# A four-layer transformer kernel on one core: the order of its steps laid down alternately backwards and forwards

## The chip, the cores and the metric

One core of one Trainium2 chip runs the whole kernel as one program. The metric is the device time of one execution in microseconds (us). The kernel before took 1387.23 us in the median of three executions (1386.0 to 1388.7). The execution that was profiled took 1388.27 us.

## The reference, cut to what matters

The input is eight batches of 256 tokens with 288 channels. Four layers follow each other. Layers 0 to 2 are transformer blocks: a layer norm that is shifted and scaled by rows made from a condition vector, attention with 16 heads of 18 channels, a projection, a second such layer norm and an MLP. Layer 0 has four experts of which each token takes two, and all four are computed. Layer 1 mixes its heads in another layout. Layer 3 is a rotation: it needs the orthogonal factor of a QR decomposition of P and the exponential of a skew matrix, both independent of x.

```
mod = silu(c) @ w_adaln + b_adaln
h = (ln(x)) * (1 + sc_msa) + sh_msa
q, k, v = split((h @ w_qkv + b_qkv))
attn = softmax(q k^T * hd ** (-0.5));  o = attn v;  x = x + g_msa * (o @ w_proj + b_proj)
xn = (ln(x)) * (1 + sc_mlp) + sh_mlp
hmid = gelu(xn @ w1 + b1);  eo = hmid @ w2 + b2;  x = x + g_mlp * sum_e cw_e * eo_e
...
U, _ = qr(P);  R = expm(A(cond));  z = x @ U;  out = x + (z @ R - z) @ U^T
```

## The kernel before

The program is not written in the order in which it runs. Python generators (`prep`, `attend`, `finish`, `up`, `down`, `householder` and others) emit **steps** with `do(lane, kind, cost, ...)`. A lane is an engine: pe, dve, act, pool, or sp, the queue that issues nearly all transfers. A step is a few instructions of one engine, with a cost in the planner's own table and the list of steps that it depends on. The dependencies include the reuse of buffers and PSUM banks, which are dealt out while the steps are emitted, so they are fixed before any reordering.

When all 4,768 steps are known, `by_readiness` deals them out once more to the five lanes: again and again it takes the lane that could start a step soonest, and on a lane the step that is ready, with the lowest `index` where several are ready within 0.1 us. Here `index` is the place in the emitted order. Steps that raise the same semaphore keep their order, and so do all steps that use an activation table. The result is five fixed lists, and each engine works through its own in order; a step that is not ready holds up everything behind it on its engine.

The kinds that matter here. `ln_stats`, `ln_aggr` (dve, L1760 and L1765), `ln_eps`, `ln_pow`, `ln_mean` (pool, L2258 to L2269) and `ln_z` (act, L2112) are a layer norm; `xb_T` (pe, L1451 and L1452) turns it, and `full`, `m_hi`, `m_lo` (dve or act or pool; L1741 or L2106, L1747, L1754 to L1756) write it to `XT` in two f16 parts. `qkv_mm` (pe, L1424) and `up_mm` (pe, L1577, up to 14 matmuls) read `XT`. `top_mm` (pe, L1529) makes scores whose row maxima `top` reduces (dve, L1845, 16 for a batch); `top_T`, `top_out` and `top_row` (pe; act; sp, L2388) send them back as a row of `QT`, and only then can the scores `s_mm` (pe, L1544) start. `down_mm` (pe, L1584 to L1589) is the MLP's second product, in three pieces for each of four 128-token tiles n0 to n3; `down_gate` (dve, L1920) and `x_add` (pool, L2285) add it to x. `cond_mm`, `cond_add` and `cond_T` (pe L1441, dve L1699, pe L1434) make the condition's rows. `w_lo`, `w2_lo` (dve) split weights into two f16 parts. `w2_in` (sp, L2364) loads the second MLP weight and `w_keep` (sp, L2370) stores split weights. The QR decomposition is 64 rounds of `hh_row` (sp, L2331), `hh_norm` (act), `hh_root` (pool) and `hh_step` (dve, L1965 to L1971), each dependent on the one before; it is needed only near the end of layer 2.

Of the kernel before, what the change touches and what calls it, by code (L numbers as in the profile page):

```python
# [24 lines left out]
LAT, FILL, TAB = 0.08, 0.15, 1.3  # L25
SIZES = dict(x_in=295, w_in=442, cond_in=345, w2_in=442, w_back=1400, w_keep=1400, g1_in=147, g2_in=295, tv_in=295, tv_out=295, out=295, v_in=640, wp1_in=350, p_in=74, hh_row=37)
AHEAD = 3
NEAR = 0.1
LATE = ("dconsts",)
TABLES = dict(exps="exp", t_exp="exp", g_exp="exp", gelu="gelu", silu="silu")  # L30
SPLIT = {(2, 3): [(0,), (1,)]}
SLACK, BIAS = -0.5, 0.2


def flat(x):
    if x is None:
        return
    if isinstance(x, list):
        for y in x:
            yield from flat(y)  # L40
    else:
        yield x
# [14 lines left out]
def ends(x):  # L57
    return max((s.end for s in flat(x)), default=0.0)
# [79 lines left out]
def by_readiness(lanes, lands):  # L138


    queues, table = [], None
    for lane in lanes:
        some = {}
        for k, st in enumerate(lane.steps):
            st.index, st.end = k + 100000 * (st.kind in LATE), None
            name = "table" if st.kind in TABLES else id(st.sem)
            some.setdefault(name, deque()).append(st)
        queues.append(list(some.values()))
        lane.steps, lane.clock = [], 0.0
    while True:  # L150
        best = None
        for lane, some in zip(lanes, queues):
            mine = None
            for qu in some:
                if qu and all(x.end is not None for x in qu[0].deps):
                    begin = max(lane.clock, max((x.end for x in qu[0].deps), default=0.0) + LAT)
                    key = (begin if begin > lane.clock + NEAR else lane.clock, qu[0].index)
                    if mine is None or key < mine[0]:
                        mine = key, begin, qu
            if mine and (best is None or mine[1] < best[0]):  # L160
                best = mine[1], lane, mine[2]
        if best is None:
            return
        begin, lane, qu = best
        st = qu.popleft()
        if st.kind in TABLES and TABLES[st.kind] != table:
            table, begin = TABLES[st.kind], begin + TAB
        lane.clock = begin + st.cost
        st.end = lands(st, lane.clock)
        lane.steps.append(st)  # L170


def part(g, n):
# [12 lines left out]
def program(nc, I, out, scr_ada, scr_v, scr_o, scr_w1, scr_w2):  # L186
    ctx = ExitStack()
    with ctx:
# [5 lines left out]
        def sem(name):  # L194
            if name not in sems:
                sems[name] = ctx.enter_context(nc.semaphore("s_" + name))
                counts[name] = 0
            return sems[name]

        wire = Wire()  # L200

        def lands(st, at):
            return (wire.land(st.kb, at) + (2.0 if st.kind == "hh_row" else 0.0)) if st.kb else at + (FILL if st.lane is pe else 0.0)

        pe, dve, act, pool, sp = (Lane(n) for n in ("pe", "dve", "act", "pool", "sp"))
        newest = [0.0]

        def do(lane, kind, cost, raises=None, incs=1, **fields):
            name = raises or kind
            s = sem(name)  # L210
            st = Step(kind, s, counts[name], counts[name] + incs, fields)
            counts[name] += incs
            lane.clock = max(lane.clock, max((ends(v) for v in fields.values() if isinstance(v, (Step, list))), default=0.0) + LAT) + cost
            st.kb, st.lane = SIZES.get(kind, 8) if incs >= 16 else 0, lane
            st.end = lands(st, lane.clock)
            newest[0] = max(newest[0], st.end)
            st.cost, st.deps = cost, [x for v in fields.values() if isinstance(v, (Step, list, tuple)) for x in flat(v) if isinstance(x, Step)]
            lane.steps.append(st)
            return st
# [8 lines left out]
        table = [None]  # L228
# [116 lines left out]

        consts = do(pool, "consts", 3.2, incs=1)
        zeros = do(dve, "zeros", 0.4)
        xt_ones = do(pool, "xt_ones", 5.5, incs=7)
        dconsts = do(dve, "dconsts", 4.4, after=consts)
        c_in = do(sp, "c_in", 0.1, incs=16)  # L350

# [901 lines left out]
        class Stream:  # L1253


            def __init__(self):
                self.todo, order = [], [0, 1, 2, 3]
                for L in range(3):
                    for c in range(4):
                        for e in order if L == 0 else [0]:  # L1260
                            for vs in SPLIT.get((L, c), [(0, 1)]):
                                self.todo.append((L, e, c, vs))
# [115 lines left out]
        ends_ = Line(chain(*(chain(*[wp_load(L)] * (L > 0), *(chain(settle_tokens(b) if L == 1 else settle(L, b), finish(L, b)) for b in range(B))) for L in range(3))), 0.5)  # L1378
        deal([Line(householder(), 4), loads, attends, ends_, tops, preps, bg, *(Line(rotated(k), 5) for k in range(2))])

        wire.clock = 0.0
        by_readiness([pe, dve, act, pool, sp], lands)

# [1082 lines left out]
def make(nc, arrays):  # L2468
    args = {k: nc.dram_tensor(f"in_{k}", a.shape, mybir.dt.from_np(a.dtype), kind="ExternalInput").ap() for k, a in arrays.items()}
    out = nc.dram_tensor("out_0", (B * T, C), F32, kind="ExternalOutput").ap()  # L2470
    scr_ada = nc.dram_tensor("scr_ada", (3, B, 6 * C), F32, kind="Internal").ap()
    scr_v = nc.dram_tensor("scr_v", (B, 11 * C), F32, kind="Internal").ap()
    scr_o = nc.dram_tensor("scr_o", (B, T, C), F32, kind="Internal").ap()
    scr_w1 = nc.dram_tensor("scr_w1", (NE, 128, 5, HID), F16, kind="Internal").ap()
    scr_w2 = nc.dram_tensor("scr_w2", (NE, 128, 19, C), F16, kind="Internal").ap()
    program(nc, args, out, scr_ada, scr_v, scr_o, scr_w1, scr_w2)
# [11 lines left out]
```

## Time and profile before

| | |
|---|---|
| median of three executions | 1387.23 us |
| profiled execution: its time | 1388.27 us |
| profiled execution: span from first to last instruction | 1386.1 us |
| PE busy | 1296.8 us (94%) |
| DVE busy | 899.0 us (65%) |
| ACT busy | 784.3 us (57%) |
| POOL busy | 444.5 us (32%) |
| mean granted TensorE clock | 0.980 |

PE is the matmul engine, DVE the vector engine, ACT the scalar engine, POOL GpSimd, SP the queue of transfers. The clock is given as a share of full speed, so 0.5 is its lower level, 1.2 GHz of 2.4. The median is 1.04 us below the profiled execution.

### The profile page before, as it was taken

The page shows a single profiled execution, that of the slowest core. Times are in us where ns is not written, and L with a number is a line of the kernel's source. Part 1 is how long each engine was busy: PE and PEld are TensorE (multiplying, and loading weights), DVE is VectorE, ACT ScalarE, POOL GpSimd, SP SyncE. Part 2 cuts the span into 40 slices and gives each one's busy share as a digit, 9 for nine tenths or more (in the row PEclk, how much of TensorE's full clock was granted, in tenths as well). Part 3 has the DMA queues.
Part 4 walks back from the last instruction along what each step waited for, and adds up shares of the span by engine and source line. Part 5 has one row for each costly group of instructions (what it writes and reads, how often), then busy time and mean ns, then how long its engine had stood idle before and what let it go on. Part 6 is the DMA issues. An engine that isn't in the chain of part 4 may idle for free.

```text
span 1386.1 us, 33182 instructions
## 1 busy us (share of the span) xinstructions
PE 1296.8 (94%) x13225; PEld 946.5 (68%) x13225; DVE 899.0 (65%) x1983; ACT 784.3 (57%) x1565; POOL 444.5 (32%) x817
## 2 busy tenths in 40 slices
PE   5687999999999899999998999899998999999998
PEld 3343756777777688777887778787675767676775
DVE  5787887767686574666537654675665855776454
ACT  3665558677666342455337344666454676756653
POOL 4122425335243432323433333223331314231210
PEclk9788999999999999999999999999999999999999
DMA  8413154554543323232324323322000020000001
GB/s 232 114 31 73 38 145 115 141 143 121 144 98 70 89 58 86 32 69 94 94 49 75 69 57 123 99 41 66 5 14 2 14 56 3 14 6 15 2 29 52
DMA packets 81935, 96.20 MB, mean 69 GB/s; under 512 B 40077, under 2 KB 74998, under 8 KB 78454
## 3 DMA queue, kind: packets, MB, share of 16 engines
q1 hardware_dynamic: 81510, 93.79, 27.5%
q8 instruction: 105, 1.72, 0.5%
q14 instruction: 48, 0.39, 0.1%
q10 hardware_dynamic: 272, 0.29, 0.1%
HBM read 73.22 MB, written 16.38 MB: 65 GB/s over the span
## 4 chain that ended last, share of the span: by engine, by line
PE 74%; DVE 12%; issue 5%; ACT 3%; DMA 3%; POOL 3%; SPq 1%; DVEq 0%; POOLq 0%; ACTq 0%
PE P L1577 18%; PE P L1424 12%; PE P L1587 7%; PE P L1589 7%; PE P L1588 7%; DVE NM L1845 5%; PE P L1553 4%; PE P L1544 2%; PE P L1520 2%; PE P L1451 2%; DMA QT<-MT 1%; PE P L1441 1%; PE P L1598 1%; PE P L1464 1%; PE P L1584 1%
## 5 line engine op out<-in xcount | busy, mean ns | idle before, releaser
L1577 PE MATMUL P<-XT,W 128*128 128x256 f16 x3024 | 351.5, 273 | 6.6 <-ACT FULL L2106 3.6
L1577 PEld LDWEIGHTS P<-XT,W 128*128 128x128 f16 x3024 | 289.8, 98 | 57.0 <-issue 12.6
L2285 POOL TENSOR_TENSOR X<-X,TM 128x288 f32<-128x288 f32 x144 | 124.3, 865 | 497.6 <-DVE TM L1920 352.4
L1587 PE MATMUL P<-W,H 128*128 128x288 f16 x864 | 247.5, 286 | 0.0
L1589 PE MATMUL P<-W,H 128*128 128x288 f16 x864 | 247.1, 286 | 0.0
L1588 PE MATMUL P<-W,H 128*128 128x288 f16 x864 | 247.1, 286 | 0.0
L2192 ACT ACTIVATE G<-P 128x512 f32<-128x512 f32 (+1 forms) x240 | 133.2, 555 | 171.7 <-PE P L1577 163.2
L2181 ACT ACTIVATE ARENA<-P 128x512 f32<-128x512 f32 x256 | 135.1, 599 | 72.7 <-PE P L1544 72.1
L1845 DVE TENSOR_REDUCE NM<-P 128x2 f16<-128x512 f32 x256 | 159.5, 686 | 11.8 <-PE P L1529 11.4
L1424 PE MATMUL P<-WQ,XT 128*128 128x288 f16 x1008 | 145.6, 296 | 11.3 <-DVE XT L1756 5.1
L2290 POOL TENSOR_TENSOR H<-G,H 128x512 f16<-128x512 f32 (+1 forms) x97 | 105.7, 1095 | 128.5 <-ACT H L2193 126.2
L2193 ACT ACTIVATE H<-P 128x512 f16<-128x512 f32 (+1 forms) x240 | 132.7, 553 | 0.0
L1914 DVE TENSOR_TENSOR H<-G,H 128x512 f16<-128x512 f32 (+1 forms) x143 | 92.0, 654 | 61.7 <-ACT H L2193 60.9
L1424 PEld LDWEIGHTS P<-WQ,XT 128*128 128x128 f16 x1008 | 96.7, 101 | 47.8 <-issue 18.9
L1587 PEld LDWEIGHTS P<-W,H 128*128 128x128 f16 x864 | 84.5, 98 | 25.9 <-issue 5.2
L1589 PEld LDWEIGHTS P<-W,H 128*128 128x128 f16 x864 | 84.5, 98 | 21.3
L1588 PEld LDWEIGHTS P<-W,H 128*128 128x128 f16 x864 | 84.6, 98 | 20.6
L2301 POOL TENSOR_SCALAR N<-HQS 64x1 f32<-64x1 f32 x64 | 19.0, 296 | 183.4 <-ACT HQS L2198 183.2
L2198 ACT ACTIVATE HQS<-HQS 64x288 f32<-64x288 f32 (+31 forms) x64 | 26.4, 413 | 86.4 <-DMA HQS<-AT 86.2
L1553 PE MATMUL P<-ARENA,V 128*32 128x256 f32 x1024 | 70.4, 392 | 3.7 <-ACT ARENA L2181 3.5
L1920 DVE SCALAR_TENSOR_TENSOR TM<-P,CW,G 128x288 f32<-128x288 f32 x64 | 32.7, 511 | 59.0 <-PE P L1589 59.0
L2106 ACT ACTIVATE FULL<-P,SC 128x256 f32<-128x256 f32 (+1 forms) x93 | 44.9, 558 | 39.9 <-PE P L1452 39.5
(304 smaller groups left out, 2132.8 us busy)
## 6 DMA issues: line engine op xcount, KB each, us to landing
W<-scr_w SPq DMA_DIRECT2D x9, 1440.0 KB, 6.2
W<-scr_w SPq DMA_DIRECT2D x9, 1368.0 KB, 6.0
scr_w<-W SPq DMA_DIRECT2D x4, 1440.0 KB, 5.9
scr_w<-W SPq DMA_DIRECT2D x4, 1368.0 KB, 5.8
STG<-in_L_w SPq DMA_DIRECT2D x8, 576.0 KB, 4.8
STG<-in_L_w SPq DMA_DIRECT2D x9, 432.0 KB, 3.4
STG<-in_L_WT SPq DMA_DIRECT2D x11, 324.0 KB, 4.4
G<-scr_ada SPq DMA_DIRECT2D x24, 144.0 KB, 3.0
```

The costliest lines, as they stand in the source:

```text
L1424: ins = e.matmul(o, l, r, start=k == 0, stop=k == len(pairs_) - 1)
L1553: ins = e.matmul(bank(st)[32 * i:32 * i + 32, at], V32[u][:, kt, 4 * g + i, :], E32[s][:, i, kt * 256:(kt + 1) * 256], start=kt == 0, stop ...
L1577: ins = e.matmul(bank(st)[:, 256 * k:256 * k + 256], W1[:, w, m * 128:(m + 1) * 128], XT[:, x, at:at + 256], start=i == 0, stop=i == 6)
L1587: e.matmul(o, hi, W2[:, 2 * m, :], start=False, stop=False)
L1588: e.matmul(o, hi, W2[:, 2 * m + 1, :], start=False, stop=False)
L1589: ins = e.matmul(o, lo, W2[:, 2 * m, :], start=False, stop=m == 8)
L1845: e.tensor_reduce(NM[:, :, st["par"], st["c"]], bank(st).rearrange("p (n k) -> p n k", n=2), AX.X, ALU.max, negate=True).then_inc(st.sem)
L2181: e.activation(E32[st["s"]][:, st["h"], :], bank(st), ACT.Exp).then_inc(st.sem)
L2192: e.activation(g32, bank(st)[:, 0:n], fn, scale=1.0 / WS)
L2193: e.activation(hi, bank(st)[:, 0:n].rearrange("p (m t) -> p m t", t=256), fn, scale=1.0 / WS).then_inc(st.sem)
L2285: e.tensor_tensor(X[:, t, :], X[:, t, :], TM[st["k"]][:, :], ALU.add).then_inc(st.sem)
L2290: e.tensor_tensor(lo, g32.rearrange("p (m t) -> p m t", t=256), hi, ALU.subtract).then_inc(st.sem)
```

## The change

The single call of `by_readiness` is replaced by `improved`. It lays the steps down forwards as before, then `from_the_end` lays the same steps down backwards: it begins with steps on which nothing waits, and gives each step an `index` that says how far from the end it stands at the latest. The next forward pass takes these as its `index`. There are twelve forward passes, and the five lists of the pass with the shortest planned length on pe are kept. `xt_ones` gets `consts` as a dependency; on pool it stands behind it in both kernels. No step's content, cost or buffer changes.

```diff
+TIMES = 12
...
-            st.index, st.end = k + 100000 * (st.kind in LATE), None
+            st.end = None
...
-        st.end = lands(st, lane.clock)
+        st.end, st.done = lands(st, lane.clock), lane.clock
...
+def from_the_end(lanes):
+    queues, then, late = [], {}, {}
+    for lane in lanes:
+        some = {}
+        for st in reversed(lane.steps):
+            name = "table" if st.kind in TABLES else id(st.sem)
+            some.setdefault(name, deque()).append(st)
+            for x in st.deps:
+                then.setdefault(id(x), []).append(st)
+        queues.append(list(some.values()))
+    clocks = [0.0] * len(lanes)
+    while True:
+        best = None
+        for k, some in enumerate(queues):
+            mine = None
+            for qu in some:
+                if qu and all(id(x) in late for x in then.get(id(qu[0]), [])):
+                    st = qu[0]
+                    begin = max(clocks[k], max((late[id(x)] + LAT + st.end - st.done for x in then.get(id(st), [])), default=0.0))
+                    key = (begin if begin > clocks[k] + NEAR else clocks[k], -st.done)
+                    if mine is None or key < mine[0]:
+                        mine = key, begin, qu
+            if mine and (best is None or mine[1] < best[0]):
+                best = mine[1], k, mine[2]
+        if best is None:
+            return
+        begin, k, qu = best
+        st = qu.popleft()
+        clocks[k] = late[id(st)] = begin + st.cost
+        st.index = -clocks[k]
+
+def improved(lanes, lands, wire):
+    for lane in lanes:
+        for k, st in enumerate(lane.steps):
+            st.index = k + 100000 * (st.kind in LATE)
+    best = None
+    for _ in range(TIMES):
+        wire.clock = 0.0
+        by_readiness(lanes, lands)
+        if best is None or lanes[0].clock < best[0]:
+            best = lanes[0].clock, [list(lane.steps) for lane in lanes]
+        from_the_end(lanes)
+    for lane, steps in zip(lanes, best[1]):
+        lane.steps, lane.clock = steps, best[0]
...
-        xt_ones = do(pool, "xt_ones", 5.5, incs=7)
+        xt_ones = do(pool, "xt_ones", 5.5, incs=7, after=consts)
...
-        wire.clock = 0.0
-        by_readiness([pe, dve, act, pool, sp], lands)
+        improved([pe, dve, act, pool, sp], lands, wire)
```

The first forward pass of `improved` is the order of before, and the lists that come out differ, so a later pass was kept. Of the 1,498 steps on pe 1,075 keep their place and the others move by 1.7 places on average. On dve the mean over all steps is 5.4 places, above all because the 64 `hh_step` move 52 places later on average. On sp the `hh_row` move 8 places later. Line numbers of the changed kernel are 50 higher.

**Place 1, dve, the program's start.** In the kernel before, behind the constants (OSM is the first `cond_add`, ST and MV a layer norm's statistics, WQ weight splits of `w_lo`):

```order
L1699 SCALAR_TENSOR_TENSOR OSM<-P,PLUS,STG 64x288
L1760 BN_STATS ST<-X 128x6
L1705 SCALAR_TENSOR_TENSOR WQ<-STG,WQ 128x288
L1705 SCALAR_TENSOR_TENSOR WQ<-STG,WQ 128x576
L1765 BN_AGGR MV<-ST 128x2
L1760 BN_STATS ST<-X 128x6
L1705 SCALAR_TENSOR_TENSOR WQ<-H,WQ 128x288
L1705 SCALAR_TENSOR_TENSOR WQ<-H,WQ 128x576
L1712 SCALAR_TENSOR_TENSOR WQ<-H,WQ 64x288
L1765 BN_AGGR MV<-ST 128x2
```

In the changed kernel, from the same place:

```order
L1810 BN_STATS ST<-X 128x6
L1815 BN_AGGR MV<-ST 128x2
L1810 BN_STATS ST<-X 128x6
L1815 BN_AGGR MV<-ST 128x2
L1749 SCALAR_TENSOR_TENSOR OSM<-P,PLUS,STG 64x288
L1755 SCALAR_TENSOR_TENSOR WQ<-STG,WQ 128x288
L1755 SCALAR_TENSOR_TENSOR WQ<-STG,WQ 128x576
L1755 SCALAR_TENSOR_TENSOR WQ<-H,WQ 128x288
L1755 SCALAR_TENSOR_TENSOR WQ<-H,WQ 128x576
L1762 SCALAR_TENSOR_TENSOR WQ<-H,WQ 64x288
```

The statistics of the first batch now stand ahead of the first condition rows and of all weight splits.

**Place 2, sp, the first batch's maxima row.** In the kernel before (HQS is `hh_row`, the two QT rows are `top_row`, H is `w2_in`):

```order
L2378 DMA G<-scr_ada 128x288
L2383 DMA G<-scr_ada 128x2x288
L2331 DMA HQS<-AT 64x1x287
L2388 DMA QT<-MT 1x8x256
L2389 DMA QT<-MT 1x8x256
L2364 DMA H<-in_L_w 128x3x288 x2
```

In the changed kernel:

```order
L2398 DMA scr_ada<-OSM 8x288
L2381 DMA HQS<-AT 64x1x288
L2414 DMA H<-in_L_w 128x3x288 x2
L2438 DMA QT<-MT 1x8x256
L2439 DMA QT<-MT 1x8x256
L2414 DMA H<-in_L_w 128x3x288
```

The second `hh_row` has gone from ahead of the maxima row, and two loads of the MLP's second weight have come ahead of it.

**Place 3, pe, where layer 0's expert loop goes from tokens 512 to 1023 to the next quarter.** In the kernel before the last pieces of `down_mm` run one behind the other, then:

```order
L1589 MATMUL P<-W,H 128x288
L1451 MATMUL P<-IDF,ARENA 128x128 x2
L1452 MATMUL P<-IDF,ARENA 32x128
L1451 MATMUL P<-IDF,ARENA 128x128 x2
L1452 MATMUL P<-IDF,ARENA 32x128
L1587 MATMUL P<-W,H 128x288
L1588 MATMUL P<-W,H 128x288
L1589 MATMUL P<-W,H 128x288
L1577 MATMUL P<-XT,W 128x256 x14
L1424 MATMUL P<-WQ,XT 128x288 x42
```

In the changed kernel three of the five `up_mm` of the last half stand behind the `down_mm` of n0 and n1, ahead of those of n2:

```order
L1638 MATMUL P<-W,H 128x288
L1639 MATMUL P<-W,H 128x288
L1627 MATMUL P<-XT,W 128x256 x35
L1634 MATMUL P<-W,ONES 128x288
L1637 MATMUL P<-W,H 128x288
```

and `xb_T` stands ahead of all of n3:

```order
L1639 MATMUL P<-W,H 128x288
L1501 MATMUL P<-IDF,ARENA 128x128 x2
L1502 MATMUL P<-IDF,ARENA 32x128
L1501 MATMUL P<-IDF,ARENA 128x128 x2
L1502 MATMUL P<-IDF,ARENA 32x128
L1634 MATMUL P<-W,ONES 128x288
L1637 MATMUL P<-W,H 128x288
```

Between the end of n1, on which the layer norm depends, and `xb_T`, 35 matmuls of `up_mm` were added. The same stands at the next two quarters, the last time with 49 matmuls and with the following `up_mm` moved behind the projections of layer 1.

## Rows read from the trace of the kernel before

**Rows 1.** Windows: busy us of each engine (instructions), granted clock, DMA share, GB/s.

```profile
0.00:35.00 35.00, 19.37 (x130) 11.18 (x132) 20.14 (x59) 12.69 (x27) 14.43 (x40) 1.00 0.85 230
35.00:145.00 110.00, 81.22 (x773) 44.12 (x768) 87.68 (x187) 67.43 (x134) 26.13 (x61) 0.81 0.30 69
145.00:460.00 315.00, 304.96 (x3113) 220.35 (x3112) 232.40 (x522) 214.07 (x427) 130.62 (x230) 1.00 0.45 112
460.00:1000.00 540.00, 521.68 (x5747) 411.00 (x5745) 328.87 (x736) 258.92 (x537) 175.85 (x353) 1.00 0.30 70
1000.00:1386.00 386.00, 369.57 (x3473) 259.86 (x3471) 229.92 (x481) 231.21 (x442) 97.44 (x133) 0.99 0.06 19
```

**Rows 2.** Timeline, DVE, 0 to 50 us: start, us, what, [idle before <- releaser].

```profile
10.36 0.51 DVE L1699 SCALAR_TENSOR_TENSOR OSM<-P,PLUS,STG 64x288 f32<-64x288 f32 x1 [3.03 <-PE P L1441]
...
14.25 0.18 DVE L1765 BATCH_NORM_AGGREGATE MV<-ST 128x2 f32<-128x6 f32 x1
...
35.11 9.65 DVE L1845 TENSOR_REDUCE NM<-P 128x2 f16<-128x512 f32 x16
```

**Rows 3.** Timeline, POOL, 0 to 50 us.

```profile
14.52 0.79 POOL L2258 TENSOR_SCALAR NMS<-MV 128x2 f32<-128x2 f32 x1 [3.61 <-DVE MV L1765]
...
16.46 0.20 POOL L2269 TENSOR_TENSOR RS<-NMS,RS 128x2 f32<-128x2 f32 x1
```

**Rows 4.** Timeline, PE, 0 to 150 us.

```profile
7.23 3.09 PE L1441 MATMUL P<-STG,CS 96*32 96x288 f32 x12 [7.23 <-DMA STG<-in_L_w_adaln]
...
17.89 0.69 PE L1451 MATMUL P<-IDF,ARENA 128*128 128x128 f32 x2 [6.32 <-ACT ARENA L2113]
...
19.36 3.10 PE L1441 MATMUL P<-H,CS 96*32 96x288 f32 x12
...
24.42 4.26 PE L1424 MATMUL P<-WQ,XT 128*128 128x288 f16 x21 [0.83 <-issue]
...
82.86 1.46 PE L1544 MATMUL P<-QT,KT 64*128 64x256 f16 x12 [2.97 <-DMA QT<-MT]
...
104.75 0.44 PE L1451 MATMUL P<-IDF,ARENA 128*128 128x128 f32 x2 [1.31 <-DVE ARENA L1862]
...
119.00 1.84 PE L1424 MATMUL P<-WQ,XT 128*128 128x288 f16 x7 [2.19 <-DVE XT L1756]
```

**Rows 5.** Chain that ended last, 0 to 60 us: start, us, what.

```profile
46.86 0.48 SPq L2331
...
47.44 0.73 SPq L2388
...
48.21 3.47 DMA QT<-MT
```

**Rows 6.** Transfers issued, 0 to 60 us: KB of each, us to landing.

```profile
H<-in_L_w SPq DMA_DIRECT2D x3, 432.0 KB, 5.0
```

**Rows 7.** The page, part 6: transfers issued.

```profile
scr_w<-W SPq DMA_DIRECT2D x4, 1440.0 KB, 5.9
```

**Rows 8.** Timeline, DVE, 100 to 120 us.

```profile
101.09 1.06 DVE L1723 SCALAR_TENSOR_TENSOR W<-H,W 128x864 f16<-128x864 f32 x1
...
116.29 0.44 DVE L1965 CUSTOM_DVE_ANT_0 HQS<-HQS,AT 64x284 f32<-64x284 f32 x1
...
117.52 0.68 DVE L1754 TENSOR_TENSOR XT<-FULL,XT 128x512 f16<-128x512 f32 x1
```

**Rows 9.** Waits of PE, 150 to 1000 us: total, times, longest.

```profile
PE P L1577 <- ACT FULL L2106: 3.6, 3, 1.3
PE P L1424 <- DVE XT L1756: 2.9, 3, 1.2
...
PE P L1464 <- issue: 1.7, 1, 1.7
```

**Rows 10.** Timeline, POOL, 555 to 580 us.

```profile
564.39 0.79 POOL L2285 TENSOR_TENSOR X<-X,TM 128x288 f32<-128x288 f32 x1 [1.73 <-DVE TM L1920]
```

**Rows 11.** The page, part 5, the largest group: busy, mean of one.

```profile
L1577 PE MATMUL P<-XT,W 128*128 128x256 f16 x3024 | 351.5, 273 | 6.6 <-ACT FULL L2106 3.6
```


## The prediction, on record before the changed kernel ran

> **What bounds the kernel now.** I read the windows first. PE is busy 1296.8 of 1386.1 us, and its idle time by stretch is span minus busy [rows 1]: 15.6 us up to 35, 28.8 us from 35 to 145, 10.0 to 460, 18.3 to 1000 and 16.4 to the end, 89.2 us in all. So PE sets the time nearly everywhere, half of what it loses lies in the first 145 us, and a new order can give back only idle time and what the clock loses. The same rows show the clock: 0.81 from 35 to 145, 0.99 to 1.00 elsewhere. At 81.2 us busy, the share below the full level is worth 15.4 us.
>
> Then I read PE's timeline and what ends its waits. Between 35 and 145 us DVE is busy 87.7 of 110 us, more than PE, and 9.65 us of it is one block of row maxima [rows 1, 2]. There PE waits for maxima, for the row that comes back by DMA (2.97 us) and for `XT` parts from DVE (2.19 us) [rows 4]. Behind 145 us the waits are few; those of a kind are three for `FULL`, 3.6 us, and three for `XT`, 2.9 us [rows 9], each pair at one crossing from one group of 512 tokens to the next in layer 0.
>
> **The change part by part.** Nothing is added or taken from any engine, so each term is a wait that shrinks or appears.
>
> *The start.* DVE idles 3.03 us up to 10.36 waiting for PE's first `cond_mm`, with the first batch's statistics behind it; these end at 14.25+0.18 [rows 2]. POOL stands idle 3.61 us up to 14.52 and needs until 16.66 for its three steps [rows 3]; PE waits 6.32 us up to 17.89 for what comes out [rows 4]. Place 1 puts the statistics ahead, into DVE's idle time. POOL is then free at 10.91 (14.52-3.61), and its 2.14 us end at 13.05, 3.6 us earlier. I take 3.0, since `ln_z` now stands behind `cond_cols` and a weight split on ACT. The first `cond_mm` gets a 432 KB load ahead of its bias: at the stretch's 230 GB/s [rows 1] up to 1.9 us later. It needed until 10.32, so until 12.2, and its columns are wanted only once `xb_T` has run, at about 16. That cover hides it. Next, `m_lo` of this batch stands behind the second `cond_add` now, which must wait for `cond_mm` to end at 22.46 (19.36+3.10) [rows 4]; in the new order it stands ahead. From `xb_T` at 17.89 to the first `qkv_mm` at 24.42 it takes 6.5 us; without that wait about 5.1. Together the projections start 4.4 us earlier; `cond_T` now stands among them (0.5 us), so the first maxima come 3.9 us earlier. Bounds: 1.5 (only `ln_z` moves, half) to 5.0.
>
> *The first maxima row.* `hh_row` holds the queue for `hh_step` until 46.86 and the row is issued at 47.44 [rows 5]. The change takes that `hh_step` and `hh_row` away from there (up to 0.7 us gained), but puts two `w2_in` ahead of the row (Place 2), 432 KB each. The row lands 3.5 us after its second half is issued; behind 864 KB at 230 GB/s it would wait up to 3.8 us more, less the head start of the loads. A 432 KB load needs 5.0 us by itself [rows 6], much of it no bandwidth. I take a loss of 1.0, bounds -0.7 and 3.8; one `qkv_mm` more stands ahead of the scores and fills part of it. Sum so far 2.9 us gained.
>
> The Trainium skill, "DMA: Bandwidth & Descriptors", section "Queues, rings and completion order", says that on each DMA engine descriptors are consumed in ring order. By that rule the row would bear the full 3.8 us, and the first maxima's 3.9 us would be spent up to here; no row of this trace has a small row directly behind such loads.
>
> *The second and third batch, 65 to 120 us.* DVE is the limit here. Of the second block of maxima the new order takes out one `hh_step` (1.2 us, as 116.29 to 117.52 [rows 8]) and an `x_lo`, and puts in a `w2_lo` (1.06 us, as at 101.09 in the same rows); I set the last two against each other: 1.2 us gained. Ahead of the third block an `hh_step` leaves the place before `av_rec`, for which PE waits 1.31 us at 104.75, and the next leaves the place before `m_lo` (117.52), for which PE waits 2.19 us at 119.00 [rows 4, 8]; `m_lo` also comes before a `proj_gate`. At most 1.31 and 1.6: I take 2.5. Two `w_keep` now stand ahead of two maxima rows in the queue, 1440 KB and 5.9 us each [rows 7]; both are ready some 15 us before those rows, which hides them; uncovered, each costs up to 5.9 us. With less idle time some of the 15.4 us of clock comes back; I take 2.0 (0 to 5), in proportion to a fifth of the 28.8 us of idle time less, rounded down. The head gives 2.9+1.2+2.5+2.0 = 8.6, say 9 us since two moves were set at nothing, bounds 1 and 14.
>
> *The three crossings in layer 0.* At the first, the last `x_add` of the tile pair runs at 564.39 [rows 10], and from there the layer norm, `xb_T`, `FULL` and `XT` are late for PE by 1.2 and 1.2 us. Place 3 puts 35 matmuls of `up_mm` between this chain's start and PE's need, at 351.5/3024 = 0.116 us each [rows 11] 4.1 us: more than the 2.4 us that were missing. The third crossing gets 49 of them, and the 1.7 us wait [rows 9] may go too. The sum of the waits is 3.6+2.9 = 6.5 us, 8.2 with the last. Against it, `down_mm` of n2 now follows directly on the last `up_mm`, whose `gelu` and `h_lo` were covered by n0 and n1 before; its first piece reads only early parts, and I allow 0.4 us for each crossing. Gain 5.0 us, bounds 1 and 8.
>
> *Everywhere else* steps have moved by one to three places on PE, and `hh_step` stands later on DVE, `hh_norm` on ACT. The decomposition then ends later, but PE needs its result only near the end of layer 2, and `v_T` there keeps its place; some 200 us remain. The 10.0, 16.4 and remaining 11.8 us of idle time can shrink or grow. The planner's durations are not the chip's, and a tighter order has less play: I take 1.0 us lost, bounds -8 and 6.
>
> Sum: 9+5-1 = 13 us. Against the profiled execution 1388.27-13 = 1375.3, its span 1373.1; the median is 1.04 us lower, so **1374 us**.
>
> **The rivals.**
>
> *Half of it is given back*: the early start is met by the queue (Place 2), and a small wait appears at each crossing where `h_lo` is late. For it speaks that ACT and DVE deliver each `up_mm` only just in time. Head 4, crossings 3: 1387-7 = 1380 us.
>
> *Nothing comes of it*: PE's work between 145 and 460 us waits for weight loads that start no earlier, so that an early head turns into a wait there. The DMA share is 0.45 at 112 GB/s, and PE idles only 10.0 of 315 us [rows 1]: against it, since loads are not the limit now. 1386 us.
>
> *More*: the scattered waits close as well and the clock holds its full level through the head (8 us of 15.4 back): 1387-13-10 = 1364 us.
>
> *Slower*: the large transfers moved ahead of the first three maxima rows. If the two `w2_in` cost 3.8 us and each `w_keep` its full 5.9 us, that is 15.6 us, and the clock costs as it does now in that stretch, 15.4 us for 28.8 us of idle time, so 8 us more. With the other head gains (3.9+1.2+2.5) and the crossings (5) that leaves 1387+23.6-12.6 = 1398 us. It decides when a `w_keep` is issued less than 6 us before a maxima row. Against it: only three of the 24 such rows got a larger transfer ahead of them.
>
> The Trainium skill, "TensorE: Matmul & The Clock Gate", Part 1, says the clock follows how busy the array has been; the trace agrees as far as it goes, with 0.81 in the stretch where PE idles 26% and 1.00 where it idles 3%.
>
> **How the numbers follow.** The forecast of 13 us has 0.50, half of it 0.24, nothing 0.10, more 0.09, slower 0.07. The forecast's own range is 1367 to 1380. The whole range of 1364 to 1384 leaves out the slower case, nothing, and a little beyond the case of more. A measurement of this kernel can tell about 0.2% (2.8 us) from no change, that is below 1384.4 or above 1390.0. Faster: 0.50+0.23+0.09 = 0.82; within: 0.10+0.01 = 0.11; slower: 0.07.
>
> **What would show it.** The first `qkv_mm` starts near 20 us instead of 24.42, the first block of maxima near 31 instead of 35.11. Idle time of PE from 35 to 145 us is near 23 instead of 28.8 and the clock is above 0.83. The three waits for `FULL` with `XT` behind them are gone or under 0.5 us. The scores of the first batch start near 49 us; if they start at 51.7 or later, the loads ahead of the row took the gain. The prediction is wrong if new waits at the `down_mm` behind an `up_mm`, or of `s_mm` for `QT`, add up to more than 5 us, or if PE's idle time behind 145 us shrinks by more than 15.

## The result, and the profile after

The changed kernel takes 1352.26 us (median of 4 executions, 1350.45 to 1354.26) against 1387.97 for the kernel before on the same chip (4 executions): a ratio of 0.9745, 95% interval 0.9725 to 0.9764. It is 36 us faster; 13 were forecast, and the time lies outside the range. The profiled execution took 1351.46 us, its span is 1349.7 us against 1386.1, the mean granted clock 0.989 against 0.980.

The changed kernel's windows, cut as in [rows 1] (us, busy of PE, its weight loads, DVE, ACT, POOL; clock, DMA share, GB/s):

```profile
0.00:35.00 35.00, 21.32 (x149) 11.52 (x149) 23.48 (x65) 12.88 (x31) 13.81 (x40) 1.00 0.85 225
35.00:145.00 110.00, 82.19 (x820) 49.92 (x821) 86.07 (x189) 70.51 (x137) 22.45 (x53) 0.88 0.31 78
145.00:460.00 315.00, 310.68 (x3265) 225.03 (x3266) 235.09 (x523) 214.09 (x423) 127.55 (x232) 1.00 0.47 117
460.00:1000.00 540.00, 534.21 (x5836) 418.65 (x5829) 344.95 (x761) 270.19 (x561) 189.52 (x367) 1.00 0.29 67
1000.00:1349.00 349.00, 335.98 (x3169) 237.94 (x3166) 215.28 (x450) 215.35 (x414) 87.73 (x126) 1.00 0.07 20
```

PE's idle time (span less busy) is 13.7, 27.8, 4.3, 5.8 and, with the last 0.7 us of the span, 13.7 us: 65.3 in all against 89.2, 24 less. PE's busy time is 12.4 us less (1284.4 against 1296.8). Most of that is the clock: in the stretches at the lower level PE was busy for 39.4 us before and for 19.0 us after, and half of each, 19.7 and 9.5 us, is what the level cost, so 10.2 less. Idle and busy time together are the 36. The profiled pair shows a large share for the clock: the four executions of the changed kernel were granted 0.984 to 0.989, and the kernel before, profiled at 0.980, was granted 0.979 to 0.984 in its executions beside the later runs, mostly 0.982 or 0.983. What does not fit the forecast is already seen here: the stretch from 35 to 145 us, where half the gain was expected, idles nearly as long as before (27.8 against 28.8 us), and the two stretches from 145 to 1000 idle 18.2 us less.

Fixed cuts mix a gain with the work that it moved. So the next windows are cut in both kernels at the same `up_mm` matmuls (the first one where the first scores for the maxima start, since no `up_mm` has run by then). First before, then after:

```profile
34.60:144.30 109.70, 80.92 (x776) 43.97 (x774) 87.31 (x186) 67.43 (x134) 26.13 (x61) 0.81 0.31 69
144.30:274.00 129.70, 122.89 (x1185) 87.00 (x1185) 101.38 (x224) 86.44 (x164) 52.51 (x91) 0.99 0.44 115
274.00:445.70 171.70, 170.06 (x1797) 124.54 (x1795) 119.12 (x275) 117.95 (x238) 68.55 (x127) 1.00 0.47 117
445.70:502.20 56.50, 51.57 (x613) 36.87 (x610) 36.45 (x90) 20.76 (x50) 21.41 (x42) 0.97 0.33 82
...
953.30:1143.80 190.50, 180.54 (x1764) 129.36 (x1761) 124.53 (x246) 114.72 (x213) 55.05 (x78) 0.98 0.07 18
1143.80:1386.00 242.20, 233.39 (x2138) 164.48 (x2135) 139.72 (x307) 142.79 (x281) 60.01 (x86) 1.00 0.06 17
```

```profile
31.50:136.80 105.30, 76.25 (x773) 43.78 (x773) 82.45 (x173) 66.92 (x132) 20.77 (x51) 0.87 0.32 81
136.80:257.30 120.50, 119.80 (x1185) 86.64 (x1184) 95.60 (x217) 85.71 (x160) 49.06 (x81) 1.00 0.46 123
257.30:429.00 171.70, 169.59 (x1797) 124.96 (x1795) 125.67 (x282) 120.10 (x242) 68.97 (x131) 1.00 0.49 118
429.00:479.20 50.20, 48.70 (x582) 34.74 (x581) 33.98 (x76) 19.21 (x45) 18.44 (x37) 1.00 0.32 90
...
924.10:1106.40 182.30, 178.47 (x1765) 127.89 (x1762) 127.20 (x254) 116.07 (x216) 54.10 (x82) 1.00 0.08 19
1106.40:1349.70 243.30, 232.47 (x2138) 164.25 (x2135) 141.77 (x309) 142.11 (x281) 60.01 (x86) 1.00 0.05 17
```

The gain of a segment is the difference of its second column. The start (0 to 34.6 in the kernel before, 0 to 31.5 after) gained 3.1 us and the head 4.4; from 144 to 274 us 9.2; nothing to 446; 6.3 to 502; 8.2 from 953 to 1144; nothing from there on. The stretch left out, 502 to 953 us before and 479 to 924 after, holds the three crossings of layer 0 and gained 6.2. The sum is 36.3 (the last segment lost 1.1). Two of these segments do not hold the same work: 32 small matmuls `P<-EY` stand ahead of the cut at 502 in the kernel before and behind it (479) in the changed one, as the counts 613 and 582 show, and they are worth some 1.4 us. So about 5 of the 6.3 us are a gain (3.4 of idle time, 1.6 of clock), and the crossings gained 7.6: their idle time fell from 12.6 to 4.9 us.

The waits of PE in the second segment, before (total, times, longest), and after, where these two lines are all:

```profile
PE P L1544 <- DVE LG L1871: 1.8, 1, 1.8
PE P L1577 <- DVE NM L1845: 1.5, 1, 1.5
PE P L1553 <- ACT ARENA L2181: 1.2, 3, 0.5
PE P L1561 <- ACT OT L2173: 0.7, 1, 0.7
```

```profile
PE P L1634 <- ACT ARENA L2231: 0.3, 1, 0.3
PE P L1634 <- DVE NM L1895: 0.2, 1, 0.2
```

None of these had been counted singly in the forecast: small waits, each another line's. (Idle time in this segment fell by 6.1 us, from 6.8 to 0.7; the clock gave 1.4 of the 9.2, and the other 1.7 stand in the profile as less busy time of PE.) The group of [rows 11] in the page after shows that the three waits for `FULL` are gone:

```profile
L1627 PE MATMUL P<-XT,W 128*128 128x256 f16 x3024 | 352.1, 273 | 0.3 <-DVE NM L1895 0.2
```

The head, as in [rows 4]: PE's timeline of the changed kernel from the start (start, us, what, idle before and its releaser):

```profile
9.31 3.09 PE L1491 MATMUL P<-STG,CS 96*32 96x288 f32 x12 [9.31 <-DMA STG<-in_L_b_adaln]
15.38 0.69 PE L1501 MATMUL P<-IDF,ARENA 128*128 128x128 f32 x2 [1.71 <-ACT ARENA L2163]
...
20.64 4.36 PE L1474 MATMUL P<-WQ,XT 128*128 128x288 f16 x21 [0.69 <-issue]
...
48.02 0.83 PE L1594 MATMUL P<-QT,KT 64*128 64x256 f16 x12
...
101.24 0.44 PE L1501 MATMUL P<-IDF,ARENA 128*128 128x128 f32 x2 [1.27 <-DVE ARENA L1912]
...
106.71 0.66 PE L1501 MATMUL P<-IDF,ARENA 128*128 128x128 f32 x2 [3.28 <-DVE NM L1895]
...
114.38 1.88 PE L1474 MATMUL P<-WQ,XT 128*128 128x288 f16 x14 [1.07 <-DVE XT L1806]
```

`cond_mm` starts 2.1 us later than in the kernel before, `xb_T` 2.5 us earlier, the first `qkv_mm` 3.8 us earlier.

### The profile page after: what moved, and what is told of

Same layout as the page of the kernel before. It is cut to its first block, busy times and chain, and to the rows that moved or that the text cites. A ratio compares the mean times of both kernels' runs of the same rounds, so it can differ in the third digit from the quotient of the medians.

```text
span 1349.7 us, 33186 instructions
## 1 busy us (share of the span) xinstructions
PE 1284.4 (95%) x13225; PEld 943.1 (70%) x13225; DVE 904.9 (67%) x1983; ACT 783.0 (58%) x1565; POOL 441.1 (33%) x817
## 4 chain that ended last, share of the span: by engine, by line
PE 80%; DVE 8%; ACT 4%; issue 3%; DMA 2%; POOL 1%; SPq 1%; DVEq 0%; ACTq 0%; POOLq 0%
PE P L1627 21%; PE P L1474 13%; PE P L1637 7%; PE P L1639 7%; PE P L1638 7%; DVE NM L1895 4%; PE P L1603 4%; PE P L1501 2%; PE P L1594 2%; PE P L1570 2%; PE P L1491 2%; PE P L1579 1%; PE P L1648 1%; PE P L1634 1%; PE P L1557 1%
## 5 line engine op out<-in xcount | busy, mean ns | idle before, releaser
L1627 PEld LDWEIGHTS P<-XT,W 128*128 128x128 f16 x3024 | 289.1, 98 | 48.6 <-issue 10.2
L1895 DVE TENSOR_REDUCE NM<-P 128x2 f16<-128x512 f32 x256 | 159.3, 685 | 14.4 <-PE P L1579 13.9
L1964 DVE TENSOR_TENSOR H<-G,H 128x512 f16<-128x512 f32 (+1 forms) x143 | 95.5, 680 | 51.2 <-ACT H L2243 50.3
```

The costliest lines, as they stand in the source:

```text
L1627: ins = e.matmul(bank(st)[:, 256 * k:256 * k + 256], W1[:, w, m * 128:(m + 1) * 128], XT[:, x, at:at + 256], start=i == 0, stop=i == 6)
L1895: e.tensor_reduce(NM[:, :, st["par"], st["c"]], bank(st).rearrange("p (n k) -> p n k", n=2), AX.X, ALU.max, negate=True).then_inc(st.sem)
```

## The experiments

Twelve kernels, each beside the kernel before on the same chip. "Gained" is always measured between the same `up_mm` matmuls against the kernel before, by the cuts above. The segments are those of the one profiled execution, the times the median of four to ten. Lines of these kernels lie a few further down than in the changed one. A round of the decomposition is counted where its `hh_step` starts: by the end of the head (144.3 us in the kernel before, 136.8 in the changed one) the kernel before has run 6 and the changed one 4, by the next cut (274 and 257.3) 15 and 11.

**1. Two passes in place of twelve.** Is it the rule, or the best of twelve draws?

```diff
-TIMES = 12
+TIMES = 2
```

> TIMES = 2: one backward pass and one forward pass behind it, instead of twelve forward passes. Theory A (the gain is in the rule itself, that a step is ranked by how far from the end it must stand): nearly all of the 35.7 us is there, 1352 to 1356 us. Theory B (the gain comes from trying many orders and keeping a lucky one): a good part is missing, 1365 us or more.

Measured 1358.5 us, ratio 0.9774 (0.9747 to 0.98), above the range of theory A by 2.5 us and far from theory B. One backward pass gives 30 of the 36 us, in the same places: 8.1 us from 144 to 274, 6.0 to 502.

**2. Only the decomposition later.** The forward pass of before, with the Householder kinds behind everything else that is ready.

```diff
-LATE = ("dconsts",)
+LATE = ("dconsts", "hh_row", "hh_norm", "hh_root", "hh_step")
...
-TIMES = 12
+TIMES = 1
```

> The order of before with one thing changed: the householder's steps (hh_row, hh_norm, hh_root, hh_step) get the last rank, so that they run only where nothing else is ready. Theory H (the householder's steps stood in the way of DVE, ACT, POOL and sp in the order of before, and moving them away is the gain): 1360 us or less. Rival (the gain needs the ranks of all steps): at most a few us, 1380 to 1388. My own terms for the head (hh_step out of three places and one hh_row) would give about 4 us, 1384.

Measured 1385.42 us, ratio 0.9970 (0.9956 to 0.9984). It gains 3.8 us in the head and 0.7 from 144 to 274, where the waits of 1.8 us for `LG` and 1.5 for `NM` stand as before. By the cut at 274 it has run 12 rounds, about as few as the changed kernel (11). So the rival came true: making the decomposition lazy does not by itself give the gain.

**3. The changed kernel with the decomposition first.** Its lists dealt once more with the Householder steps ahead of all.

```diff
+        for lane in (pe, dve, act, pool, sp):
+            for k, st in enumerate(lane.steps):
+                st.index = k - 100000 * st.kind.startswith("hh_")
+        wire.clock = 0.0
+        by_readiness([pe, dve, act, pool, sp], lands)
```

> The changed kernel with one thing undone: in its final order the householder's steps get the first rank again, so that each runs as soon as it can; all other steps keep their ranks. Theory H: most of the gain is lost, 1370 us or more. Rival: PE keeps what it has, since DVE, ACT and POOL are 65%, 58% and 33% busy, 1352 to 1358.

Measured 1374.02 us, ratio 0.9884 (0.9861 to 0.9907), 22 us slower than the changed kernel, as theory H had it. By the matmul that the changed kernel reaches at 257.3 it has run 22 rounds instead of 11 and is 14.9 us behind. Its windows to there:

```profile
31.30:143.10 111.80, 81.09 (x775) 45.53 (x775) 93.13 (x209) 69.11 (x144) 30.15 (x81) 0.81 0.40 80
```

```profile
143.10:272.20 129.10, 122.61 (x1183) 86.87 (x1183) 103.57 (x236) 87.06 (x170) 57.34 (x109) 0.98 0.48 117
```

DVE is 10.7 and 8.0 us busier than in the changed kernel and the clock is back at 0.81. Yet the crossings and the stretch from 953 to 1144 keep their gain, and 4.8 of the 6.3 us before 502 stay: those are not the decomposition's. This run does not undo the change, though: with 11 rounds in the head and 22 by the second cut it is far ahead of the kernel before too (6 and 15). It shows what eleven rounds too many cost, not what the four that the changed kernel puts off are worth.

**4. New order at the front, old behind it.** Each list is cut at 150 us of the plan's own time.

```diff
+    for lane, a, b in zip(lanes, best[1], old):
+        lane.steps = [st for st in a if ends_new[id(st)] < 150.0] + [st for st in b if ends_new[id(st)] >= 150.0]
```

> The new order for the first 150 us of the plan, the order of before for all that is left. If the gain of each stretch is its own, only the head's 7.5 us remain, and 1380 us comes out. If the new head hands work over so that the next stretch (145 to 274 us, 9.1 us gained there) runs better in the old order too, it is 1371 us or less. If the seam costs a wait, 1382 to 1386.

Measured 1403.36 us, ratio 1.0101 (1.0086 to 1.0116). The front gains 2.6 and 4.2 us as in the changed kernel; then comes one wait at the seam,

```profile
PE P L1582 <- ACT KT L2221: 17.3, 1, 17.3
```

which is far more than the seam was expected to cost (1403 us against 1382 to 1386). Behind it, from 502 to 1025 us, each segment is within 0.1 us of the kernel before. PE arrives there 14 to 16 us late, not early, so the run does not show whether an early head helps later; it shows that the old lists take their old time wherever they start.

**5 and 6. PE's new list with the helpers by the old order, and the reverse.** One list is kept as it is, the others are dealt out again around it by the other kernel's ranks.

```diff
+            name = "pinned" if lane.name in pinned else "table" if st.kind in TABLES else id(st.sem)
...
+    for lane, a, b in zip(lanes, best[1], old):
+        for k, st in enumerate(b):
+            st.index = k
+        lane.steps = a if lane.name in ("pe",) else b
+    by_readiness(lanes, lands, ("pe",))
```

(The second has `old` and `best[1]` exchanged.)

> PE's list is that of the changed kernel, word for word; the other four lanes are dealt out by the ranks of before. Theory P (the gain is in PE's own order, the helpers have room): 1352 to 1360 us. Theory J (the ranks pay only on all engines together, since PE meets each result as soon as the helpers' order brings it): most of the gain is lost, 1375 us or more.

> The reverse: PE's list is that of before, word for word; the other four lanes are dealt out by the ranks of the changed kernel. Theory P: no gain, about 1388 us. Theory J: no gain either and perhaps a loss, 1385 to 1397. Theory H (moving the helpers' work off the critical places is the gain): 1370 us or less.

Measured 1385.56 us, ratio 0.9978 (0.9965 to 0.9991), and 1382.55 us, ratio 0.9954 (0.9936 to 0.9972). PE's list alone brings the first two crossings in full (2.8 and 2.2 us) and 3.0 us before 502, and loses 2.7 from 274 to 446. The helpers' order alone brings the start (2.7), 4.7 us from 144 to 274, 2.5 before 502 and 5.6 from 1025 to 1144, nothing at the crossings, and loses 6.5 us in the head and 5.3 from 274 to 446. For the first, theory J holds; the second lies below J's range and far above H's. (The 3.0 us before 502 of PE's list hold the 1.4 us of moved matmuls.) About 3 and 6 us alone, 36 together: most of the gain comes only when PE's list and the others fit each other.

**7, 9 and 10. The crossings by hand.** In PE's list of the kernel before the last three `up_mm` steps of each quarter go behind n0 and n1 (7), `xb_T` goes ahead of n3 (10), or both (9); the helpers keep the old ranks.

```diff
+            a[k - 2:k + 7] = a[k + 1:k + 7] + a[k - 2:k + 1]
...
+            t = next(i for i in range(k + 7, k + 14) if a[i].kind == "xb_T")
+            n3 = next(i for i in range(k + 7, k + 14) if a[i].kind == "down_mm" and a[i]["n"] == 3)
+            a.insert(n3, a.pop(t))
```

> The order of before with my own crossing term alone: on PE, at the three crossings between groups of 512 tokens in layer 0, the last three up_mm of the second half run behind the down_mm of n0 and n1 instead of ahead of them; the other lanes are dealt out by the ranks of before. By my term: 2.4, 2.4 and 1.7 us of waits go, less 0.4 each, 1383 us. If the down_mm behind the last up_mm waits for h_lo, 1387 us or more.

> The kernel before with two hand edits at each of the three crossings: the first up_mm matmuls stand between n0 and n1 of the next layer on TensorE, and xb_T stands ahead of n3. Theory (two swaps are needed for the cover that the prediction priced): the waits for FULL and XT at the crossings go, 2.9 + 2.2 + about 1 us, so 1382 to 1383 us. Rival (the crossing is bound by VectorE's chain, not by what TensorE has to do meanwhile): 1387 to 1389 us, with the waits under other names.

> The kernel before with xb_T ahead of n3 at the three crossings and nothing else. Theory: with no matmul of the layer left between n0 and n1, TensorE waits as long as before, 3.6 us three times for FULL, so 1387 to 1389 us. Rival (xb_T's place alone is the whole of it): 1384 or less.

What is expected of the last two describes the edits loosely: the three `up_mm` stand behind n0 and n1, not between them, and the 3.6 us for `FULL` are the sum of three waits. In the kernel of 7 L1642 is `up_mm`, in that of 10 L1518 is `xb_T`.

The first swap alone: 1388.86 us, ratio 0.9994 (0.9977 to 1.0011), no change where 1383 was expected; 0.7 us gained at each of two crossings, and the wait is where it was:

```profile
PE P L1642 <- ACT FULL L2171: 3.7, 3, 1.3
```

`xb_T` alone: 1393.13 us, ratio 1.0035 (1.002 to 1.005), slower. The expected 1387 to 1389 is missed on the far side: `xb_T` now waits itself, up to 2.4 us, and every later step of n3 stands behind it. Of the 5.3 us lost between 502 and 953 in its profiled execution 2.2 are idle time and 3.4 are clock: it falls to its lower level at 727 and at 887 us, which it does not in the kernel before.

```profile
PE P L1518 <- ACT ARENA L2180: 7.8, 5, 2.4
```

Both: 1383.83 us, ratio 0.9966 (0.9954 to 0.9978), 5.5 us faster than the kernel before, close to the 1382 to 1383 expected; 2.5 and 2.4 us gained at the first two crossings and nothing at the third. Windows of the first crossing, before and with both swaps:

```profile
544.70:593.70 49.00, 46.45 (x469) 38.59 (x467) 31.67 (x76) 26.75 (x60) 17.45 (x44) 1.00 0.31 49
```

```profile
544.80:591.20 46.40, 46.13 (x468) 38.45 (x466) 31.73 (x76) 26.78 (x59) 19.44 (x44) 1.00 0.34 51
```

PE's idle time there is 2.6 us before and 0.3 after. Two moves that bring 0 and -5 us alone bring 5 together.

**8. The new ranks for the front only, all dealt anew.** As experiment 4, but the steps behind 150 us are dealt out from the ranks of before, so that no seam is forced.

```diff
+            st.index = fresh[x] - 100000 if ends_new[x] < 150.0 else place[x]
```

> The ranks of the changed kernel for the steps of the first 150 us of the plan, the ranks of before for all others, dealt out anew, so that no fixed list waits at a seam as in the run before. If the head's gain keeps: 7 us, 1381. If the householder's rounds that the head puts off (5 done by its end instead of 7) come back as work in the next stretch: half or more is given back, 1385 to 1389.

Measured 1381.48 us, ratio 0.9944 (0.9926 to 0.9962). It gains 4.4 and 6.0 us by the end of the head, more than the changed kernel, and gives back 5.9 from 144 to 274, with 11 rounds of the decomposition there where the changed kernel has 7 and the kernel before 9:

```profile
133.90:269.30 135.40, 125.85 (x1183) 88.43 (x1183) 100.52 (x234) 86.83 (x168) 54.80 (x100) 0.95 0.46 111
```

The time is the 1381 of the case that the head's gain keeps, but by luck: the head gained more than was expected, and half of it was given back, as the other case had it. Of the 5.9 us 2.7 are idle time, and the clock there is 0.95 where it was 0.99.

**11. The decomposition held back further.** In the plan it may not begin before the 64th block `top`.

```diff
+        tops_ = [st for st in dve.steps if st.kind == "top"]
+        next(st for st in sp.steps if st.kind == "p_in").deps.append(tops_[64 - 1])
```

> The changed kernel, with the Householder chain (p_in and all behind it) held in the plan until the 64th top of VectorE, so that its rounds stand later than the changed kernel has them. Theory that what VectorE does ahead of 260 us costs the end one for one (1.35 us a round, 11 rounds there): 1337 to 1345 us. Rival (the changed kernel already puts rounds only where VectorE has room, TensorE idles 0.7 us in that segment, so nothing is left to gain there and only the head's 29 us of idle time could): 1349 to 1353 us.

Measured 1361.29 us, ratio 0.9800 (0.9771 to 0.9829): 9 us slower than the changed kernel. My theory of 1.35 us for every round falls, and so does the rival. No round runs in the head and 6 instead of 7 in the next segment, and both are slower than in the changed kernel:

```profile
33.50:143.50 110.00, 81.14 (x775) 44.97 (x773) 82.12 (x159) 65.00 (x122) 13.40 (x26) 0.82 0.26 76
```

DVE is no less busy than with four rounds (82.12 against 82.45 us): other instructions moved into the window, two more of the maxima among them, and some took longer, one weight split of 64x288 1.33 us where the changed kernel's takes 0.45. PE idles as long in the head as in the changed kernel (28.9 against 29.1 us), but the clock is 0.82 there instead of 0.87: waits of the same sum in other places cost some 5 us more of clock. And PE's first wait, for the transfers of the condition's weights and bias, lasts 12.1 us instead of 9.3, so the first `qkv_mm` starts at 22.18 us instead of 20.64.

**12. The shortest plan found.** The same hold at the 112th `top`, steps taken as ready within 0.2 us, 20 passes.

```diff
-NEAR = 0.1
+NEAR = 0.2
-TIMES = 12
+TIMES = 20
...
+        next(st for st in sp.steps if st.kind == "p_in").deps.append(tops_[112 - 1])
```

> The changed kernel with the chain held in the plan until the 112th top, steps taken as ready within 0.2 us instead of 0.1, and 20 passes: the shortest planned length found, 1309.4 against 1316.0 for the changed kernel. If planned and measured lengths move together as they did between the kernel before and the changed one (planned 1348.7 to 1316.0, measured 1388 to 1352), 1344 to 1347 us. Rival (a few planned us are within what the plan gets wrong): 1349 to 1356 us.

Measured 1352.52 us, ratio 0.9736 (0.9711 to 0.9762): the changed kernel's time, by another way. It gained 6.2 us in the head, with idle time there down from 28.8 to 23.3 us, and 8.6 from 144 to 274 with no round at all before 257 us, and lost 4.0 us from 1144 to 1325, where rounds run until 1128 and the clock fell once more. The planner's own sum for it is 6.6 us shorter than for the changed kernel; the chip shows none of that, as the rival had it.

## Why the prediction was right and wrong

*The start: right.* Forecast were first maxima 3.9 us earlier; they start at 31.91 instead of 35.11, 3.2 earlier. `cond_mm` started 2.1 us late behind the 432 KB load, as said, and its cover held: it ends at 12.40 and `xb_T` starts at 15.38. The first `qkv_mm` was 3.8 us earlier against 4.4.

*The first maxima row: the loss of 1.0 did not come.* SP's queue in the changed kernel:

```profile
42.33 0.92 SPq L2414 DMA_DIRECT2D H<-in_L_w  x2
43.44 0.75 SPq L2438 DMA_DIRECT2D QT<-MT  x1
44.23 0.66 SPq L2439 DMA_DIRECT2D QT<-MT  x1
```

The scores start at 48.02, 4.6 us after the row is issued, where they took 4.3 before (47.44 [rows 5] to 51.73), and PE was busy until then, so the row bore 0.3 us at most from what stood ahead of it. The scores are 3.7 us earlier (forecast 2.9, that is about 49 us). The price of 3.8 us was wrong in its rate. The two loads landed 3.3 and 4.0 us after their issue, by 46.9 us, and from 44 to 46 us the engines moved 347 and 392 GB/s, not 230; so their bytes were through within the 3.5 us that such a row needs by itself. The rule of ring order ("DMA: Bandwidth & Descriptors", section "Queues, rings and completion order", of the Trainium skill) is neither borne out nor refuted by this: the row's data can have gone behind both loads without being late, and the profile does not show in what order the engines took them.

*The second and third batch: half wrong.* Forecast were 3.7 us of waits and 2.0 of clock. The wait for `XT` shrank from 2.19 to 1.07 us, that of `xb_T` for `ARENA` stayed (1.31 and 1.27), and a new one of 3.28 us came, of `xb_T` for the end of a block of maxima. The waits for the row that comes back, 4.8 us of `s_mm` for `QT`, are all gone, and others, for maxima and for `ARENA` from ACT, have taken their place: idle time in this segment did not fall, 28.8 and 29.1 us. The 4.4 us gained there are all clock, 0.81 to 0.87. The head gave 7.5 instead of 9, by another sum: I had put too much on waits and too little on the clock.

*The crossings: right in size at the first two, incomplete in mechanism.* 5.0 forecast; the first two gained 2.8 and 2.2 us, and with the third and the steady parts it is 7.6 (6.2 between the cuts, which includes the matmuls that moved in). The three waits of `up_mm` for `FULL` are gone. But the working put the whole cover on the 35 matmuls; experiment 7 has them and gains 1.4 us, 10 has the other move and loses, and only 9, both, gains 5. `down_mm` of n2 right behind `up_mm` did not become a wait: 0.4 us in all for `H`.

*"Everywhere else steps have moved by one to three places on PE ... I take 1.0 us lost, bounds -8 and 6": this is the step that failed.* It gained some 21 us (9.2 + 5 + 8.2, less 1.1 lost at the end), more than twice what any reading of its bounds allows (a gain of 6 or of 8), and the text had named the sign: idle time behind 145 us less by more than 15 (it fell from 44.8 to 23.8). Two errors were in it. I took the mean shift of a step as the size of the effect, though waits of 0.5 to 2 us, none of which was looked at singly, closed when the lists were laid anew; and I gave the clock a term in the head alone, though behind it another 5.7 us (1.4, 1.6 and 2.7) were lost at the lower level before, and none after. What of the gain belongs to the decomposition is open. Its order can cost 15 us by 257 us (experiment 3, with 22 rounds there), but the kernel before had 15 rounds there and the changed one 11, and experiment 2 with 12 gained 0.7 us in the segment in which the changed kernel gained 9.2. The 5 and the 8.2 are independent of it (experiment 3 keeps them for the most part). The lists alone bring little: of the 9.2 PE's new list gives 1.0 and the helpers' order 4.7; of the 5 they give 1.6 and 2.5; of the 8.2 the helpers' order gives 5.6 and PE's list 1.0 (5 and 6).

*The rivals.* "More" had the right mechanism, scattered waits closing and the clock with them, and only 10 us and 0.09 for it. "Slower" priced the transfers moved ahead; none cost more than 0.3 us at the first row, and the waits of PE for the transfer of `QT` sum to 0.3 us in the whole changed kernel, where they were 10.3. The 15.4 us of clock in the head, which the prediction's clock terms use, take a mean over time for one over busy time: PE was busy for 27.4 us at the lower level in the five stretches up to 123 us and for 1.4 from 143.6 to 145, which cost 14.4.

*Open.* The order of experiment 11 loses 9 us against that of the changed kernel, and its rounds do not explain it: in its profiled execution some 2 us are lost in the start, 5 in the head, about all of it clock, and 4.5 from 144 to 274; why its waits stand where they do was not tried. And which single steps make the segment from 144 to 274 dense was not tried one by one.

## What to carry to other kernels

When each engine works through a fixed list, a new order is worth what the lists are worth together: test a move with its partner, since two that bring nothing or a loss alone may close a wait together. Price a reordering by the sum of all of PE's small waits and of the clock's dips, over a quarter of the gain in the profiled pair, and not by how far steps move; and cut both traces at the same instructions to see where it came back, with a look at the counts, since work that moved over a cut looks like a gain. A step's rank counted back from the end is a rule worth one extra pass: two passes brought 30 of the 36 us. A planned length does not tell versions within some 7 us apart (the planner's own sums, no times of the chip: 1309.4 ran as 1316.0 did, and 1313.1, that of experiment 11, ran 9 us slower).

## What the runs showed of the hardware

The clock's lower level, 1.2 GHz, was granted in eight separate stretches of the kernel before, seven of 3.4 to 7 us and one of 17, of which one at 143.6 and two more behind it; in the changed kernel in four, the last of which ends at 113 us, and for the span's last microsecond. The two late ones of the kernel before as windows:

```profile
467.90:471.30 3.40, 3.18 (x40) 1.79 (x40) 0.75 (x2) 1.52 (x5) 1.29 (x5) 0.50 0.00 0
1044.80:1051.60 6.80, 5.49 (x37) 2.85 (x38) 1.05 (x2) 4.56 (x9) 0.00 (x0) 0.50 0.00 0
```

They cost 3.18 and 5.49 times a half, 1.6 and 2.7 us, behind three waits of 0.70, 1.69 and 0.96 us (from 464 to 468 us) and two of 1.24 and 0.66 us (up to 1043.4; a third, of 2.09 us, falls into the stretch itself). The segments around them, 446 to 502 and 953 to 1144 us, are 91 and 95% busy as a whole. I had not expected that so little idle time brings the clock down there.

A dip is no fixed property of a list, and one trace does not settle it. (Stretches are again cut at the same matmuls; their times are those of the kernel before.) Between 1025 and 1144 us the profiled executions of the eight kernels whose helpers run there by the old order (the kernel before and experiments 2, 4, 5, 7, 8, 9 and 10) each show 1.4 to 3.0 us lost to the lower level (half of PE's busy time there), with 6.5 to 7.6 us of idle time; the six others, with 2.4 to 4.5 us of idle time, show none. That the new order takes this dip away is borne out so. But between 1144 and 1325 us, with 3.4 to 4.1 us of idle time in every kernel, nine of the fourteen profiled executions show a dip or two (1.7 or 3.4 us) and five do not, among them the kernel before, while experiment 4, which runs the same lists there, does. And from 144 to 274 us experiments 2, 7 and 9 kept the waits and had no dip, where the kernel before lost 1.4 us.
